# A selective-scan and FP4 feed-forward kernel: the same instructions in other slots, B rows ahead of C rows on the transfer queue

## The chip, the cores and the metric

One core of one Trainium2 chip runs the whole program. The metric is the device time in microseconds, the median of the runs shown. Engine names in the profile: PE is TensorE, DVE is VectorE, ACT is ScalarE, POOL is GpSimd, SP is SyncE, which here only issues transfers.

## The reference

A Mamba layer followed by a feed-forward layer, each with a layer norm before it and a residual after it; 16 sequences of 1024 tokens, 256 channels, f32.

```python
xz = layernorm(x) @ in_proj_w.T;  x, z = split(xz)            # 512 + 512
x = silu(causal_conv4(x) + conv_b);  xh = x as 4 heads of 128
dt_r, B, C = split(x_proj_w[h] @ xh)                          # 16 + 16 + 16 per head
delta = softplus(dt_proj_w[h] @ dt_r + dt_proj_b);  A = -exp(A_log)
s[t] = s[t-1] * exp(delta[t] * A) + (delta[t] * xh[t]) * B[t] # 16 states per channel
y[t] = sum_n s[t, n] * C[t, n];  y = (y + x * Dskip) * silu(z)
x1 = x_in + y @ out_proj_w.T
h = silu(fp4(v) @ fp4(w_gate).T) * (fp4(v) @ fp4(w_up).T)     # v = layernorm(x1), inner 704
out = x1 + fp4(h) @ fp4(w_down).T                             # fp4: blocks of 16, scaled by max/6
```

## The kernel before

**Units and tiles.** The scan work is cut into 128 units: one head (128 channels on the partitions) by 512 tokens. A unit has 16 states, and each state is one step. The norm, output and feed-forward work is cut into 128 tiles of 128 tokens. So one unit and one tile pass per 16 steps. A sequence has 8 units: four "early" ones (its first 512 tokens, whose scan starts at zero) and four "late" ones (whose scan starts at a carried state). Their VectorE scans are told apart in the profile by the operand `carry`.

**One step of the scan**, for state n (`g` counts all states): TensorE spreads B's row over the partitions into one of three PSUM banks `db` (`spread_b`, L1056), ScalarE makes the decay (`decay_of`, L486), VectorE multiplies `db` by `du` (L987) one step ahead and scans (L1008). `spread_b(g)` may write its bank only when scan g-3 is done. For the states 1, 4, 8, 11 and 14 (`BY_POOL`) the product is made by GpSimd instead (`drive`, L743): SyncE copies the B row to all partitions (`copy_b`, L404, two buffers, free again when the scan before last of its kind is done), and ScalarE puts the decay into the `db` bank. For each pair of states GpSimd multiplies the two states by C (`weigh`, L752), with the C rows copied by SyncE (`spread_c`, L392, three buffers: pair p waits for `weigh` of pair p-3). TensorE adds the products up (`sum_up`, L1071).

**The tables of slots.** Every engine runs one long loop of steps, and its `step` function lists jobs as `if w := due("scan", s):` and so on. The job is issued in the step with number s modulo 16, for the unit or tile that this many steps lie behind; jobs of one step are issued in the order of the text. Nothing else sets the order: each engine takes its list in turn and blocks on the semaphores of the job at its head. The engines' steps aren't aligned with one another except by these waits.

**Names used below.** Per unit: `in_proj` (L1186) makes x in `pbank` (two matmuls, k = 0 and 1) and z in `bank_a`; `delta` is the softplus of ScalarE (L591), and the first `in_proj` matmul waits for it since it read `pbank`; `du` (L801) is delta times the gated input, by GpSimd. Per tile: `rstd` (L733, GpSimd) makes the norm's factors, ScalarE's L581 applies the second of them, `silu_gate` (L503) comes behind it, then `delta`, then the absolute value of the second half of h (L596), which VectorE's `round_up_h` (L902) waits for. `down` (L1160) is the last matmul of the feed-forward, in three pairs.

Of the kernel before, what the change touches and what calls it, by code (L numbers as in the profile page):

```python
# [14 lines left out]
ALU = mybir.AluOpType  # L15
# [3 lines left out]
P = 128  # L19
# [122 lines left out]
def build(nc, hidden, win_t, conv_w, conv_b, xw, dtw, dt_b, a_log, dskip, wo_t, w_gate, w_up, w_down,  # L142
# [4 lines left out]
    with ExitStack() as ctx:  # L147
# [215 lines left out]
        def _(sp):  # L363
# [42 lines left out]
            def step(b, j, n):  # L406
                u, due = timetable(b, j, n)
                if t := due("post", 5):
                    wait(sp, x1_done, t.val(plus=-1))
                    sp.dma_start(xres[:, t.mod(2), :], x_tiles[t.val()]).then_inc(ld_res[t.mod(2)], 16)  # L410
                if w := due("scan", 5):
                    spread_c(w, 4)
                if w := due("scan", 0):
                    copy_b(w, 4)
                if w := due("scan", 0):
                    spread_c(w, 2)
                if t := due("norm", -16):
# [3 lines left out]
                if v := due("pre", 16):  # L421
# [5 lines left out]
                if t := due("post", 76):  # L427
                    sp.wait_ge(o_done, t.val(plus=1))
                    sp.dma_start(out_tiles[t.val()], ot[:, t.mod(2), :]).then_inc(ot_free[t.mod(2)], 16)
                if w := due("scan", 10):  # L430
                    spread_c(w, 7)
                if w := due("scan", -6):
                    copy_b(w, 1)
                if w := due("scan", 7):
                    spread_c(w, 6)
                if w := due("scan", 7):
                    copy_b(w, 14)
                if w := due("scan", -1):
                    spread_c(w, 0)
                if w := due("scan", -1):  # L440
                    spread_c(w, 1)
                if w := due("scan", 6):
                    spread_c(w, 5)
                if w := due("scan", 3):
                    copy_b(w, 8)
                if w := due("scan", 3):
                    copy_b(w, 11)
                if w := due("scan", 3):
                    spread_c(w, 3)
# [14 lines left out]
        def _(act):  # L464
# [50 lines left out]
            def step(b, j, n):  # L515
                u, due = timetable(b, j, n)
                if w := due("scan", 9):
                    decay_of(w, 15)
                if w := due("scan", 9):
                    keep_carry(w, 0)  # L520
                if w := due("scan", -7):
                    decay_of(w, 0)
                if t := due("post", 25):
                    act.wait_ge(v_norm, t.val(plus=1))
                    wait(act, h_op, t.val(2))
                    act.activation(bank_b[:, 0:DM], v2, ACT.Abs, scale=POWER).then_inc(v_abs, 1)
                if w := due("scan", 3):
                    decay_of(w, 9)
                if w := due("scan", 6):
                    decay_of(w, 10)  # L530
                if w := due("scan", 6):
                    decay_of(w, 12)
                if w := due("scan", 3):
                    decay_of(w, 4)
                if t := due("norm", 19):
# [6 lines left out]
                if t := due("post", 35):  # L542
                    silu_gate(t, 0)
                if v := due("pre", 20):
                    act.wait_ge(res_mm, v.val(2, 2))
                    wait(act, b_spread, v.val(N_DVE, -N_DVE))
                    act.activation(pieces[:, v.mod(2), :], pbank[:, :], ACT.Copy).then_inc(pieces_done, 1)
                if t := due("post", 20):
# [4 lines left out]
                                   accum_out=ve[:, 1, 0:1]).then_inc(var2_done, 1)  # L553
                if w := due("scan", 20):
# [4 lines left out]
                if due("post", 37) and not due("pre", 21):  # L559
                    act.preload_act_table_set("exp_and_others")  # L560
                if w := due("scan", 14):
                    decay_of(w, 14)
                if t := due("post", 52):
                    act.wait_ge(h_norm, t.val(plus=1))
                    wait(act, h_round, t.val(4))
                    act.wait_ge(cross_taken, min(t.val(plus=7), UNITS))
                    act.activation(cross[:, 0:HALF], hv[t.mod(2)][:, 0:HALF], ACT.Abs, scale=POWER).then_inc(h_abs, 1)
                if t := due("post", 31):
                    act.wait_ge(v_tp, t.val(plus=1))
                    wait(act, gu_mm, t.val(4))  # L570
                    act.activation(vt[:, :, :], bank_b[:, 0:DM].rearrange("p (k t) -> p k t", k=KM),
                                   ACT.Copy).then_inc(vt_done, 1)
                if t := due("norm", 15):
# [3 lines left out]
                if t := due("post", 63):  # L577
                    fetch_h(t, 0)
                if t := due("post", 20):
                    act.wait_ge(rstd_done, t.val(plus=12))  # L580
                    act.activation(v2, v2, ACT.Copy, scale=ve[:, 1, 1:2]).then_inc(v_done, 1)  # L581
                if t := due("post", 36):
                    silu_gate(t, 1)
                if w := due("scan", 20):
                    keep_carry(w, 1)
                if v := due("pre", 20):
                    h = v.mod(HEADS)
                    act.preload_act_table_set("softplus")
                    act.wait_ge(dt_mm, v.val(plus=1))
                    wait(act, du_done, v.val(plus=-1))  # L590
                    act.activation(delta[:, v.mod(2), :], pbank[:, :], ACT.Softplus,  # L591
                                   bias=dtb[:, h:h + 1]).then_inc(delta_done, 1)
                    act.preload_act_table_set("exp_and_others")
                if t := due("post", 52):
                    act.wait_ge(h_round, t.val(4, 2))
                    act.activation(cross[:, 0:HALF], hv[t.mod(2)][:, HALF:INNER], ACT.Abs, scale=POWER).then_inc(h_abs, 1)  # L596
                if w := due("scan", 7):
                    decay_of(w, 8)
                if v := due("pre", 7):
# [7 lines left out]
                    else:  # L607
                        wait(act, x_evac, v.val(2, -6))
                        act.activation(xlate[:, 0:TAPS - 1], halo[:, h, :], ACT.Copy).then_inc(x_evac, 1)
                        act.activation(xlate[:, TAPS - 1:], pbank[:, :], ACT.Copy).then_inc(x_evac, 1)  # L610
                if w := due("scan", 7):
                    decay_of(w, 13)
                if t := due("norm", -6):
# [4 lines left out]
                if w := due("scan", -6):  # L618
                    decay_of(w, 2)
                if t := due("post", 18):  # L620
                    act.wait_ge(sum2_done, t.val(plus=1))
                    wait(act, v_tp, t.val())
                    act.activation(v2, x1[:, t.mod(4), :], ACT.Identity, bias=sum2[:, 0:1],  # L623
                                   scale=-float(DM)).then_inc(centred2, 1)
                if v := due("pre", 18):
                    act.wait_ge(res_mm, v.val(2, 1))
                    act.activation(mid[:, :], pbank[:, :], ACT.Copy).then_inc(mid_done, 1)
                if w := due("scan", 2):
                    decay_of(w, 7)
                if w := due("scan", 11):  # L630
                    decay_of(w, 11)
                if t := due("norm", -5):
                    act.wait_ge(sum1_done, t.val(plus=1))
                    wait(act, xn_tp, t.val(plus=-1))
                    act.activation(xn[:, t.mod(2), 0:DM], xin[:, t.mod(2), 0:DM], ACT.Identity, bias=sum1[:, 0:1],
                                   scale=-float(DM)).then_inc(centred1, 1)
                if w := due("scan", -5):
                    decay_of(w, 3)
                if v := due("pre", 12):
# [10 lines left out]
                if w := due("scan", 0):  # L650
                    decay_of(w, 1)
                if v := due("pre", 16):
                    act.wait_ge(xd_mm, v.val(plus=1))
                    wait(act, dt_mm, v.val())
                    wait(act, res_mm, v.val(2))
                    wait(act, c_written, v.val(16))
                    wait(act, b_written, v.val(16))
# [765 lines left out]
```

## Time and profile before

| | us |
|---|---|
| median of 3 runs | 4243.98 |
| lowest and highest | 4243.51, 4249.21 |
| the profiled execution | 4253.05 |
| its span | 4251.1 |
| VectorE busy | 4060.8 (96%) |
| TensorE busy, matmuls | 3945.4 (93%) |
| GpSimd busy | 3941.9 (93%) |
| ScalarE busy | 3639.7 (86%) |

The profiled execution is one run of its own; the rows below count its span. A row of the timeline gives the start, the duration, the engine, the line and what is written from what; square brackets hold the time in which the engine had nothing to do before it, and what ended that. `x2` merges two instructions that stand next to each other. TensorE's granted clock is given as a share of full speed, 2.4 GHz.

### The profile page before, as it was taken

What the parts mean: (1) busy time and instruction counts of PE and PEld (TensorE: products, weight loads), DVE (VectorE), ACT (ScalarE), POOL (GpSimd) and SP (SyncE); (2) the same over time, 40 slices, a digit from 0 to 9 for tenths busy, and PEclk for the clock granted to TensorE, in tenths of its full rate; (3) what the DMA queues carried; (4) which work ended last, traced back from release to release, by engine and by line L of the source; (5) the groups of instructions that cost most, each with busy time, mean ns of one, the idle gap of its engine ahead of it and who ended that gap; (6) DMA issues with size and microseconds to landing.
All of it is one profiled execution on the core that took longest, in us unless ns stands there. A gap on an engine that the chain in (4) does not pass through costs nothing. (4 is left out here: it accounts for less than half of the span.)

```text
span 4251.1 us, 67554 instructions
## 1 busy us (share of the span) xinstructions
PE 3945.4 (93%) x19884; PEld 1859.3 (44%) x19884; DVE 4060.8 (96%) x5684; ACT 3639.7 (86%) x6807; POOL 3941.9 (93%) x2461
## 2 busy tenths in 40 slices
PE   4789999999999999999999999999999999999997
PEld 1234444444444444444444444444444444444445
DVE  6899999999999999999999999999999999999994
ACT  5888888888888888888888888888888888888874
POOL 5999999999999999999999999999999999999993
PEclk8999999999999999999999999999999999999999
DMA  3555555555555555555555555555555555555550
GB/s 107 200 192 192 186 187 191 186 189 188 185 187 190 188 185 191 184 189 191 188 184 191 184 187 190 185 185 190 192 183 190 188 186 190 189 186 187 183 184 23
DMA packets 307411, 772.79 MB, mean 182 GB/s; under 512 B 37734, under 2 KB 89062, under 8 KB 307046
## 3 DMA queue, kind: packets, MB, share of 16 engines
q1 hardware_dynamic: 305344, 766.31, 54.0%
q8 instruction: 162, 2.65, 0.2%
q10 hardware_dynamic: 1702, 2.16, 0.2%
q14 instruction: 203, 1.66, 0.1%
HBM read 743.16 MB, written 25.17 MB: 181 GB/s over the span
## 5 line engine op out<-in xcount | busy, mean ns | idle before, releaser
L752 POOL TENSOR_TENSOR prod<-state,cs 128x1024 f32<-128x1024 f32 x1024 | 2411.5, 2367 | 10.6 <-issue 10.3
L743 POOL TENSOR_TENSOR brow<-brow,du 128x512 f32<-128x512 f32 x640 | 817.2, 1277 | 189.6 <-DMA brow<-b_rows 179.2
L486 ACT ACTIVATE decay<-delta,aneg 128x512 f32<-128x512 f32 x1408 | 962.4, 716 | 22.5 <-DVE state L1008 20.7
L987 DVE TENSOR_TENSOR db<-db,du 128x512 f32<-128x512 f32 x1408 | 962.3, 683 | 17.8 <-PE db L1056 16.9
L1071 PE MATMUL ybank<-prod,ident 64*64 64x512 f32 x3584 | 899.3, 610 | 9.9 <-DVE hh L905 6.4
L1071 PE MATMUL cross<-prod,ident 64*64 64x512 f32 x3584 | 899.2, 610 | 0.0
L1008 DVE TENSOR_TENSOR_SCAN state<-decay,carry,db 128x512 f32<-128x512 f32 x704 | 883.1, 1263 | 0.0
L1008 DVE TENSOR_TENSOR_SCAN state<-decay,db 128x512 f32<-128x512 f32 x704 | 841.6, 1204 | 6.3 <-PE bank_b L1344 6.3
L1056 PE MATMUL db<-pieces,sel 128*128 128x512 bf16 x1408 | 541.3, 385 | 48.9 <-DVE state L1008 42.9
L486 ACT ACTIVATE db<-delta,aneg 128x512 f32<-128x512 f32 x640 | 437.8, 684 | 47.6 <-DVE state L1008 44.5
L1160 PE MATMUL bank_a<-wd,ht 128*128 128x256 f32 x1536 | 406.6, 390 | 57.7 <-ACT hh L503 56.0
L1008 DVE TENSOR_TENSOR_SCAN state<-db,carry,brow 128x512 f32<-128x512 f32 x320 | 408.1, 1275 | 9.7 <-issue 8.0
L1008 DVE TENSOR_TENSOR_SCAN state<-db,brow 128x512 f32<-128x512 f32 x320 | 388.7, 1215 | 28.4 <-issue 23.2
L1071 PEld LDWEIGHTS ybank<-prod,ident 64*64 64x64 f32 x3584 | 203.2, 133 | 472.6 <-issue 378.1
L1160 PEld LDWEIGHTS bank_a<-wd,ht 128*128 128x128 f32 x1536 | 289.3, 193 | 253.2 <-issue 223.9
L1186 PE MATMUL pbank<-xnt,win 128*128 128x512 f32 x512 | 281.2, 633 | 111.1 <-ACT delta L591 110.4
L1145 PE MATMUL bank_a<-wg,vt 128*128 128x352 f32 x1024 | 356.7, 471 | 5.2 <-DVE x L945 2.7
L1056 PEld LDWEIGHTS db<-pieces,sel 128*128 128x128 bf16 x1408 | 137.1, 97 | 505.6 <-DVE state L1008 341.1
L1112 PE MATMUL bank_b<-wu,vt 128*128 128x352 f32 x1024 | 345.5, 460 | 0.0
L581 ACT ACTIVATE v_eps<-v_eps,ve 128x256 f32<-128x256 f32 x128 | 65.2, 509 | 238.4 <-POOL ve L733 238.3
L1175 PE MATMUL bank_a<-wo,yg 128*128 128x256 f32 x1024 | 263.9, 380 | 0.0
L1112 PEld LDWEIGHTS bank_b<-wu,vt 128*128 128x128 f32 x1024 | 194.4, 190 | 134.7 <-issue 59.6
(144 smaller groups left out, 7643.7 us busy)
## 6 DMA issues: line engine op xcount, KB each, us to landing
cs<-c_rows SPq DMA_DIRECT2D x1024, 512.0 KB, 3.7
brow<-b_rows SPq DMA_DIRECT2D x640, 256.0 KB, 3.9
xin<-in_hidden SPq DMA_DIRECT2D x128, 128.0 KB, 3.8
xres<-in_hidden SPq DMA_DIRECT2D x128, 128.0 KB, 3.8
out_x<-ot SPq DMA_DIRECT2D x128, 128.0 KB, 3.9
c_rows<-xdbl SPq DMA_DIRECT2D x128, 32.0 KB, 3.4
b_rows<-xdbl SPq DMA_DIRECT2D x128, 32.0 KB, 3.2
win<-in_win_t SPq DMA_DIRECT2D x1, 1024.0 KB, 5.1
```

The lines of the kernel that those rows point to most:

```text
L486: act.activation(out, delta[:, w.mod(2), :], ACT.Exp, scale=aneg[:, w.mod(HEADS), n:n + 1]).then_inc(done, 1)
L743: pool.tensor_tensor(brow[:, s, :], brow[:, s, :], du[:, w.mod(2), :], ALU.mult).then_inc(db_pool, 1)
L752: pool.tensor_tensor(prod[:, r, :, :], state[:, 2 * p:2 * p + 2, :], cs[:, c, :, :], ALU.mult).then_inc(weighted, 1)
L987: dve.tensor_tensor(t[:, :], t[:, :], du[:, gu % 2, :], ALU.mult).then_inc(db_done, 1)
L1008: dve.tensor_tensor_scan(state[:, n, :], by, plus, start, ALU.mult, ALU.add).then_inc(scanned, 1)
L1056: pe.matmul(db[g % DB_BANKS][:, :], sel[:, gn, :], pieces[:, gu % 2, :], start=True, stop=True).then_inc(b_spread, 1)
L1071: last = pe.matmul((ybank, cross)[k][c * Q:(c + 1) * Q, :], ident[rows, rows], prod[rows, p % P_RING, k, :], start=(p == 0), stop=(k == 1 ...
L1112: last = pe.matmul(bank_b[:, 0:HALF], vt[:, k, :], wu[:, k, part * HALF:(part + 1) * HALF], start=(k == 0), stop=(k == KM - 1))
L1145: last = pe.matmul(bank_a[:, 0:HALF], vt[:, k, :], wg[:, k, part * HALF:(part + 1) * HALF], start=(k == 0), stop=(k == KM - 1))
L1160: last = pe.matmul(bank_a[:, 0:DM], ht[:, k, :], wd[:, k, :], start=(k == 0), stop=(k == KI - 1))
L1175: last = pe.matmul(bank_a[:, 0:DM], yg[:, t.mod(8) // 4, h, i * P:(i + 1) * P], wo[:, h, :], start=(h == 0), stop=(h == HEADS - 1))
L1186: return pe.matmul((pbank, bank_a)[part][:, :], win[:, k, part * DI + h * P:part * DI + (h + 1) * P], xnt[:, v.mod(8) // 4, k, :], start=( ...
```

## The change

Only the slots and the order of jobs in the tables change, on all five engines. No instruction is added or removed, and the count of steps, buffers and semaphores is the same.

A few lines of the diff stand for its kind:

```diff
# SyncE
-                if w := due("scan", 0):
-                    copy_b(w, 4)
+                if w := due("scan", -3):
+                    copy_b(w, 4)
# GpSimd
-                if v := due("pre", 26):
+                if v := due("pre", 23):
                     pool.wait_ge(delta_done, v.val(plus=1))
                     ...
-                if w := due("scan", 4):
+                if w := due("scan", 6):
                     drive(w, 8)
# TensorE
-                if v := due("pre", 6):
+                if v := due("pre", 7):
                     pe.wait_ge(xnt_done, v.div(4, 4, 4))
                     wait(pe, delta_done, v.val())
                     in_proj(v, 0, 0)
+                if v := due("pre", 7):
+                    in_proj(v, 0, 1).then_inc(x_mm, 1)
# VectorE
-                if t := due("post", 47):
+                if t := due("post", 48):
                     dve.wait_ge(h_scale, t.val(3, 2))
                     dve.reciprocal(hs[:, 1, :], hs[:, 0, :]).then_inc(h_scale, 1)
```

SyncE before, from the C rows of pair 7 (`waits weighted`, first row) to those of pair 2 of the next unit; the rows between are B row 1, the result's tile, C pairs 0 and 1, and B row 4:

```order
L392 DMA cs<-c_rows 128x1024 [waits weighted]
L404 DMA brow<-b_rows 128x512 [waits scanned,b_written]
L429 DMA out_x<-ot 128x256 [waits o_done]
L392 DMA cs<-c_rows 128x1024 [waits weighted,c_written]
L392 DMA cs<-c_rows 128x1024 [waits weighted]
L404 DMA brow<-b_rows 128x512 [waits scanned]
L392 DMA cs<-c_rows 128x1024 [waits weighted]
```

SyncE now, from B row 1 on (C pair 7 follows the result's tile, then B row 4, C pair 0, the tile of x, C pairs 1 and 2):

```order
L404 DMA brow<-b_rows 128x512 [waits scanned,b_written]
L442 DMA out_x<-ot 128x256 [waits o_done]
L392 DMA cs<-c_rows 128x1024 [waits weighted]
L404 DMA brow<-b_rows 128x512 [waits scanned]
L392 DMA cs<-c_rows 128x1024 [waits weighted,c_written]
L425 DMA xin<-in_hidden 128x256 [waits var2_done,var1_done]
L392 DMA cs<-c_rows 128x1024 [waits weighted] x2
```

B row 4 stood behind C pairs 0 and 1 of its unit, whose waits are for `weigh` of pairs 5 and 6 of the unit before; now it stands ahead of both. Likewise B row 14, which stood behind C pair 6, now stands ahead of C pairs 5 and 6.

GpSimd before, from `drive` 4 (first row) to `weigh` 3 (last row; `du` comes two places after it):

```order
L743 TENSOR_TENSOR brow<-brow,du 128x512
L770 TENSOR_TENSOR hh<-hh,hs 128x704
L752 TENSOR_TENSOR prod<-state,cs 128x1024
L733 TENSOR_TENSOR ve<-ve,minus_half 128x2
L743 TENSOR_TENSOR brow<-brow,du 128x512
L752 TENSOR_TENSOR prod<-state,cs 128x1024 x2
L743 TENSOR_TENSOR brow<-brow,du 128x512
L807 TENSOR_TENSOR v_eps<-v_eps,vs 128x256
L752 TENSOR_TENSOR prod<-state,cs 128x1024
```

GpSimd now, the same stretch:

```order
L743 TENSOR_TENSOR brow<-brow,du 128x512
L789 TENSOR_TENSOR hh<-hh,hs 128x704
L752 TENSOR_TENSOR prod<-state,cs 128x1024
L733 TENSOR_TENSOR ve<-ve,minus_half 128x2
L752 TENSOR_TENSOR prod<-state,cs 128x1024
L743 TENSOR_TENSOR brow<-brow,du 128x512
L774 TENSOR_TENSOR du<-delta,uu 128x512
L752 TENSOR_TENSOR prod<-state,cs 128x1024
L782 TENSOR_TENSOR v_eps<-v_eps,vs 128x256
L743 TENSOR_TENSOR brow<-brow,du 128x512
L752 TENSOR_TENSOR prod<-state,cs 128x1024
```

`drive` 8 moved behind `weigh` 1, `du` moved forward to directly behind it, and `drive` 11 now follows `du`, `weigh` 2 and the short product of the norm.

TensorE before, around `in_proj` into `pbank`, which waits for `delta` (the `db` rows are the spreads of states 9 and 10):

```order
L1160 MATMUL bank_a<-wd,ht 128x256 x2
L1186 MATMUL pbank<-xnt,win 128x512
L1160 MATMUL bank_a<-wd,ht 128x256 x2
L1056 MATMUL db2<-pieces,sel 128x512
L1186 MATMUL pbank<-xnt,win 128x512
L1160 MATMUL bank_a<-wd,ht 128x256 x2
L1056 MATMUL db0<-pieces,sel 128x512
```

TensorE now, the same stretch:

```order
L1160 MATMUL bank_a<-wd,ht 128x256 x2
L1186 MATMUL pbank<-xnt,win 128x512 x2
L1160 MATMUL bank_a<-wd,ht 128x256 x2
L1056 MATMUL db0<-pieces,sel 128x512
L1056 MATMUL db1<-pieces,sel 128x512
L1160 MATMUL bank_a<-wd,ht 128x256 x2
```

Both `in_proj` matmuls now stand ahead of the spread of state 9.

## Rows read from the trace of the kernel before

**Rows 1.** The page: busy time of the engines, and the group of `weigh`.
```profile
PE 3945.4 (93%) x19884; PEld 1859.3 (44%) x19884; DVE 4060.8 (96%) x5684; ACT 3639.7 (86%) x6807; POOL 3941.9 (93%) x2461
...
L752 POOL TENSOR_TENSOR prod<-state,cs 128x1024 f32<-128x1024 f32 x1024 | 2411.5, 2367 | 10.6 <-issue 10.3
```

**Rows 2.** VectorE by stretches: length, busy (count), clock, DMA share, GB/s.
```profile
0.00:300.00 300.00, 252.82 (x285) 0.92 0.52 166
300.00:3900.00 3600.00, 3520.07 (x4956) 1.00 0.56 188
4100.00:4251.00 151.00, 93.53 (x173) 0.92 0.22 71
...
2120.00:2248.00 128.00, 122.68 (x173) 0.97 0.57 187
2248.00:2376.00 128.00, 127.81 (x181) 1.00 0.56 188
```

**Rows 3.** VectorE's waits, 300 to 3900 us: total, times, longest.
```profile
DVE hw L902 <- ACT cross L596: 47.1, 78, 0.8
DVE state L1008 <- issue: 24.1, 38, 1.7
DVE db L987 <- PE db L1056: 6.4, 13, 0.8
```

**Rows 4.** GpSimd's longest wait, 300 to 3900 us.
```profile
POOL brow L743 <- DMA brow<-b_rows: 154.5, 110, 2.7
```

**Rows 5.** SyncE's issues in an early unit, timeline.
```profile
2135.51 2.59 SPq L392 DMA_DIRECT2D cs<-c_rows  x2
2138.15 0.43 SPq L404 DMA_DIRECT2D brow<-b_rows  x1
```

**Rows 6.** GpSimd in the same unit: `drive` 4 and `rstd`.
```profile
2143.00 1.27 POOL L743 TENSOR_TENSOR brow<-brow,du 128x512 f32<-128x512 f32 x1 [1.67 <-DMA brow<-b_rows]
...
2147.88 0.70 POOL L733 TENSOR_TENSOR ve<-ve,minus_half 128x2 f32<-128x2 f32 x1
```

**Rows 7.** ScalarE behind `rstd` in the same unit.
```profile
2148.61 0.51 ACT L581 ACTIVATE v_eps<-v_eps,ve 128x256 f32<-128x256 f32 x1 [2.50 <-POOL ve L733]
...
2150.89 0.69 ACT L591 ACTIVATE delta<-pbank,dtb 128x512 f32<-128x512 f32 x1
```

**Rows 8.** VectorE in that unit: scans 14 and 0, then its three waits.
```profile
2133.85 1.21 DVE L1008 TENSOR_TENSOR_SCAN state<-db,brow 128x512 f32<-128x512 f32 x1
...
2137.45 1.16 DVE L1008 TENSOR_TENSOR_SCAN state<-decay,db 128x512 f32<-128x512 f32 x1
...
2144.36 1.22 DVE L1008 TENSOR_TENSOR_SCAN state<-db,brow 128x512 f32<-128x512 f32 x1 [0.63 <-issue]
...
2153.39 0.53 DVE L902 SCALAR_TENSOR_TENSOR hw<-cross,hh 128x352 f32<-128x352 bf16 x1 [0.81 <-ACT cross L596]
...
2155.62 0.70 DVE L987 TENSOR_TENSOR db<-db,du 128x512 f32<-128x512 f32 x1 [0.85 <-PE db L1056]
```

**Rows 9.** TensorE in that unit: the matmuls that waited for `delta`.
```profile
2151.72 1.91 PE L1186 MATMUL pbank<-xnt,win 128*128 128x512 f32 x2 [1.00 <-ACT delta L591]
```

**Rows 10.** That stretch: length, busy of PE, PEld, DVE, ACT, POOL, clock, DMA.
```profile
2150.00:2158.00 8.00, 7.00 (x26) 3.75 (x28) 6.22 (x12) 6.67 (x11) 8.00 (x5) 0.79 0.53 177
```

**Rows 11.** A late unit, GpSimd: `drive` 8 and `drive` 11.
```profile
2021.48 1.27 POOL L743 TENSOR_TENSOR brow<-brow,du 128x512 f32<-128x512 f32 x1
...
2027.35 1.28 POOL L743 TENSOR_TENSOR brow<-brow,du 128x512 f32<-128x512 f32 x1
```

**Rows 12.** The same late unit, VectorE: the product of state 9, then scan 11.
```profile
2027.79 0.69 DVE L987 TENSOR_TENSOR db<-db,du 128x512 f32<-128x512 f32 x1
...
2033.77 1.27 DVE L1008 TENSOR_TENSOR_SCAN state<-db,carry,brow 128x512 f32<-128x512 f32 x1
```

**Rows 13.** The same late unit, TensorE: `in_proj` behind `delta`, the spread of state 9.
```profile
2024.55 1.10 PE L1186 MATMUL pbank<-xnt,win 128*128 128x512 f32 x2 [0.82 <-ACT delta L591]
...
2026.35 0.38 PE L1056 MATMUL db<-pieces,sel 128*128 128x512 bf16 x1
```

More of the change, by code:

```diff
@@ L516, in step @@
                 u, due = timetable(b, j, n)
[L517 to L535, printed above, removed]
+                if t := due("norm", 20):
                     act.wait_ge(xn_tp, t.val(plus=1))
@@ L558, in step @@
                     act.activation(ycross, cross[:, :], ACT.Copy).then_inc(cross_taken, 1)
[L559 to L573, printed above, removed]
+                if t := due("post", 67):
+                    fetch_h(t, 1)
+                if w := due("scan", 3):
+                    decay_of(w, 7)
+                if w := due("scan", 3):
+                    decay_of(w, 4)
+                if v := due("pre", 19):
+                    act.wait_ge(res_mm, v.val(2, 1))
+                    act.activation(mid[:, :], pbank[:, :], ACT.Copy).then_inc(mid_done, 1)
+                if w := due("scan", 0):
+                    decay_of(w, 1)
+                if t := due("norm", 16):
                     act.wait_ge(rstd_done, t.val(plus=1))
@@ L802, in step @@
                                        ALU.mult).then_inc(du_done, 1)
-                if w := due("scan", 8):
-                    drive(w, 11)
+                if w := due("scan", 5):
+                    weigh(w, 1)
+                if w := due("scan", 7):
+                    weigh(w, 2)
                 if t := due("post", 24):
@@ L809, in step @@
                 if w := due("scan", 8):
+                    drive(w, 11)
+                if t := due("post", 50):
+                    pool.wait_ge(h_scale, t.val(3, 3))
+                    hb = blocks(hv[t.mod(2)])
+                    pool.tensor_tensor(hb, hb, spread(hs[:, 1, :], INNER // BLK),
+                                       ALU.mult).then_inc(h_norm, 1)
+                if t := due("post", 58):
+                    pool.wait_ge(h_round, t.val(4, 4))
+                    hb = blocks(hv[t.mod(2)])
+                    pool.tensor_tensor(hb, hb, spread(hs[:, 0, :], INNER // BLK),
+                                       ALU.mult).then_inc(h_quant, 1)
+                if w := due("scan", 10):
+                    weigh(w, 4)
+                if w := due("scan", 3):
+                    weigh(w, 0)
+                t1, t2 = due("norm", 3), due("post", 19)
+                if t1 or t2:
+                    rstd(t1, t2)
+                if t := due("post", 28):
+                    pool.wait_ge(v_round, t.val(2, 2))
+                    pool.tensor_tensor(blocks(v2), blocks(v2), spread(vs[:, 0, :], DM // BLK),
+                                       ALU.mult).then_inc(v_quant, 1)
+                if w := due("scan", 9):
                     weigh(w, 3)
+                if w := due("scan", 1):
+                    drive(w, 4)
             def quantise(w, k):
@@ L1261, in side @@
-                if w := due("scan", 11):
-                    spread_b(w.val(NST, 13))
-                if v := due("pre", 12):
-                    in_proj(v, 1, 1).then_inc(z_mm, 1)
-                if w := due("scan", 12):
-                    sum_up(w, (2,))
-                if w := due("scan", 12):
-                    sum_up(w, (3,))
-                if t := due("post", 28):
-                    pe.wait_ge(v_quant, t.val(plus=1))
-                    if peeled and t.val() == 0:
-                        pe.wait_ge(xnt_done, 11)
-                    else:
-                        wait(pe, h_op, t.val(2))
-                    for k in range(KM):
-                        last = pe.transpose(bank_b[:, k * P:(k + 1) * P], v2_eps[:, k * P:(k + 1) * P], ident[:, :])
-                    last.then_inc(v_tp, 1)
@@ L1278, in side @@
[L1278 to L1287 removed]
+                if w := due("scan", 14):
+                    spread_b(w.val(NST, 15))
@@ new lines, in side @@
+                if v := due("pre", 14):
+                    pe.wait_ge(u_done, v.val(plus=1))
+                    pe.matmul(pbank[:, :], xws[:, v.mod(HEADS), :], uu[:, v.mod(4), :],
+                              start=True, stop=True).then_inc(xd_mm, 1)
+                if w := due("scan", -2):
+                    spread_b(w.val(NST, 0))
+                if t := due("post", 14):
+                    project(t, (1, 2, 3))
+                if w := due("scan", 9):
+                    spread_b(w.val(NST, 9))
@@ new lines, in side @@
+                if t := due("post", 64):
+                    turn_h(t, 0)
+                if w := due("scan", 16):
+                    sum_up(w, (4,))
+                if t := due("post", 71):
+                    down(t, (0, 1))
+                if v := due("pre", 7):
+                    pe.wait_ge(xnt_done, v.div(4, 4, 4))
+                    wait(pe, delta_done, v.val())
+                    in_proj(v, 0, 0)
+                if v := due("pre", 7):
+                    in_proj(v, 0, 1).then_inc(x_mm, 1)
@@ new lines, in side @@
+                if v := due("pre", 11):
+                    wait(pe, o_done, v.val(plus=-9))
+                    if v.val() < 10:
+                        wait(pe, sz_done, v.val())
+                        wait(pe, x1_done, v.val(plus=-6))
+                        wait(pe, silu_g, v.val(2, -14))
+                    in_proj(v, 1, 0)
+                if v := due("pre", 11):
+                    in_proj(v, 1, 1).then_inc(z_mm, 1)
+                if w := due("scan", 22):
+                    pe.wait_ge(cross_taken, w.val(plus=1))
+                    pe.matmul(ybank[:, :], swap[:, :], ycross, start=False, stop=True,
+                              skip_group_check=True).then_inc(joined, 1)
@@ L1314, in side @@
+                if t := due("post", 38):
+                    up(t, 1)
+                if w := due("scan", 11):
+                    sum_up(w, (2,))
+                if w := due("scan", 13):
+                    sum_up(w, (3,))
                 if t := due("post", 13):
                     project(t, (0,))
-                if w := due("scan", -3):
-                    spread_b(w.val(NST, 0))
+                if t := due("post", 29):
+                    pe.wait_ge(v_quant, t.val(plus=1))
+                    if peeled and t.val() == 0:
+                        pe.wait_ge(xnt_done, 11)
+                    else:
+                        wait(pe, h_op, t.val(2))
+                    for k in range(KM):
+                        last = pe.transpose(bank_b[:, k * P:(k + 1) * P], v2_eps[:, k * P:(k + 1) * P], ident[:, :])
+                    last.then_inc(v_tp, 1)
@@ L1319, in unit @@
+                if t := due("post", 65):
+                    turn_h(t, 1)
+                if w := due("scan", 1):
+                    spread_b(w.val(NST, 3))
             def unit(trip, j):
```

446 lines of the change are left out of this document (203 added, 243 removed).

## The prediction

> **What bounds the kernel now.** I read the page first: VectorE is busy 96% of the span, TensorE and GpSimd 93% [rows 1]. No edit removes an instruction, so a gain can only come out of VectorE's idle time, as long as VectorE stays the fullest engine. Then the stretches [rows 2]: from 300 to 3900 us VectorE works 3520.1 of 3600 us, so 79.9 us are idle there. The first 300 us hold 47.2 idle us and the last 151 us hold 57.5, both from filling and draining. The two rows of 128 us are the most telling. The one that lies mostly in early units (scans without `carry`) has 5.3 idle us in about four units, the one in late units has 0.2. Late units are full: nothing is to be had there. Early units lose 1.3 us each, and 64 of them make 85 us, which agrees with the 79.9.
>
> Next the waits of VectorE in that stretch [rows 3]: 47.1 us for ScalarE's absolute value (L596), 24.1 us at a scan that needs a GpSimd row ("issue": the profile names no releaser), 6.4 us for a spread by TensorE. Together 77.6 us. To find what starts them I followed one early unit.
>
> - SyncE issues B row 4 at 2138.15 [rows 5]. It stood behind a C transfer that waits for `weigh` of pair 6, though its own condition, scan 14 of the unit before, was met when that scan ended at 2133.85 + 1.21 = 2135.06 [rows 8].
> - GpSimd's `drive` 4 starts at 2143.00, after 1.67 us of waiting for the row [rows 6]: 4.85 us from issue to use. The wait occurs 110 times and totals 154.5 us [rows 4].
> - VectorE's scan 4 waits 0.63 us [rows 8] for it. GpSimd's `rstd` comes late by the same 1.67 us; ScalarE waits 2.50 us for it [rows 7], and everything behind on ScalarE is late: `delta`, then the absolute value, for which VectorE waits 0.81 us [rows 8].
> - TensorE waits 1.00 us for `delta`, and the two matmuls behind the wait take 1.91 us [rows 9] where the same two take 1.10 us in a late unit [rows 13]; the granted clock of that stretch is 0.79 [rows 10], a mix of the 2.4 GHz and 1.2 GHz levels, after two waits of about 1 us. So the spread of state 9 is late, and VectorE waits 0.85 us [rows 8].
>
> One late transfer thus stands at the head of all three waits.
>
> **The change part by part.**
>
> *B row 4 ahead of C pairs 0 and 1.* Its copy can go out when scan 14 ends, at about 2135.1 in that unit, since the C transfer now ahead of it (pair 7) waits for `weigh` 4, long done. With the same 4.85 us it is usable at 2139.95. GpSimd was free for it at 2143.00 - 1.67 = 2141.33. The wait of 1.67 us goes, with 1.4 us to spare. What comes late next? C pairs 0 and 1 are issued at most one issue, 0.43 us, later, and are needed two or more products later: no cost. B row 14 now waits for scan 8 ahead of C pairs 5 and 6, which are needed only by the `weigh`s after `drive` 14: no cost, and if this cover is gone it shows as a wait of `weigh` for its transfer.
>
> *GpSimd's order.* Its sum of work is the same. `drive` 8 moves behind one `weigh`, 2.37 us [rows 1]. It started at 2021.48 and ends at 2022.75, while scan 8 comes behind the product that starts at 2027.79 [rows 11, 12]: margin 5.0 us, 2.7 left. `drive` 11 ended at 2028.6 and scan 11 starts at 2033.77 [rows 11, 12]; it moves back by `du` and a short product, about 1.9 us, and 3.2 us are left. Both at nothing. `du` moves forward and now needs `delta` early: after `rstd` GpSimd has `weigh` 1 and `drive` 8, 2.37 + 1.27 = 3.6 us [rows 1, 11], before it. `delta` ended 2150.89 + 0.69 - (2147.88 + 0.70) = 3.0 us after `rstd` [rows 6, 7]. Margin 0.6 us: no cost, but thin.
>
> *TensorE's order.* Both `in_proj` matmuls now stand between `delta` and the spread of state 9. By the late unit that puts the spread about 0.9 us later behind `delta` (half of 1.10 with its overlap up to half of 1.91 at the lower clock: 0.55 to 0.96) [rows 9, 13]. The spread ended at 2026.73 and its product started at 2027.79 [rows 12, 13], a margin of 1.06 us in late units and none in early ones. But `delta` itself should come earlier against VectorE, by what GpSimd no longer waits: 1.67 us in the early unit. So the early spread gains 1.67 and gives back at most 0.96. I leave 4 of the 6.4 us of this wait in.
>
> *VectorE's order.* The reciprocal of h's scales moves from ahead of scan 0 to behind it. Scan 0 behind it took 1.16 us against 1.21 for scan 14 [rows 8]. If this small saving is lost, it costs 0.05 x 128 = 6.4 us; if it is found again elsewhere, 0. I take 3, the middle, as both are equally near. `round_up_h` of the second half now comes ahead of the gated y product, which is some 0.6 us earlier in VectorE's order, so it asks for more of ScalarE: 1.67 gained on ScalarE's chain less 0.81 that was missing and less 0.6 leaves 0.3 us to spare. I leave 8 of the 47.1 us in.
>
> *ScalarE's and the other slots.* ScalarE is busy 86% and its decays run up to six states ahead; filling and draining keep the same leads. I take 0, with -5 to +5 for the slots at the two ends, about a tenth of their 47.2 + 57.5 idle us.
>
> **The sum.** Against the profiled execution, 4253.05: the scan wait 24.1 to 2 (-22), the wait for ScalarE 47.1 to 8 (-39), the spread 6.4 to 4 (-2.4), the reciprocal +3. That makes -60.5, or 4192.6. The profiled execution is 9.1 us above the median of the runs shown, 4243.98, so the forecast there is 4183.5, rounded to 4183. All of rows 3 removed and nothing given back would be 4166; the ends -5 make it 4161.
>
> **The rivals.**
>
> *The gain is cut to half.* GpSimd needs 3941.9 / 128 = 30.8 us per unit, set-up included [rows 1], and VectorE's early unit 122.7 / 4 = 30.7 [rows 2]. Once the transfer doesn't hold it, GpSimd has nothing to catch up with, and any wait of its own reaches VectorE within the four early units. If half of the 77.6 us stay: 4244 - 39 + 3 = 4208. For it: the margins of 0.3 and 0.6 us above. Against it: late units, where VectorE needs more, give GpSimd time to get ahead again.
>
> *The wait only moves: no change.* If ScalarE takes over 0.6 us longer from `rstd` to `delta` than before, GpSimd waits at `du`. With 1 us or more of that per unit it is where it was with the transfer: 4244.
>
> *Slower, by the spread of state 9.* If `delta` doesn't come earlier against VectorE (because ScalarE's new order spends the gain), the spread is 0.55 to 0.96 us later in every unit. The early units have no margin, and 64 x 0.9 = 58 us are added: 4302; late units lie at the edge of their 1.06. It decides from a `delta` that comes less than 0.9 us earlier. For it: TensorE's waits before these matmuls come with the lower granted clock [rows 9, 10]. Against it: the source of the lateness of `delta` is the one that the change takes away. The Trainium skill, "TensorE: Matmul & The Clock Gate", section "HAM oscillation — how this bites in real kernels", says that a wait ahead of each burst of matmuls can send the array back to the low clock so that each burst starts slow; the trace agrees, with 1.91 us against 1.10. By that rule the added matmul costs its high-end price in each unit whose wait stays, and next to nothing where the wait goes.
>
> *The change doesn't do what it says.* If the B rows' 4.85 us grow with another load on the queue, `drive` 4 waits on; over 1.4 us more are needed. I count this with no change.
>
> **How the numbers follow.** Forecast (4165 to 4205) 0.60; half (4205 to 4235) 0.16, so faster 0.76. Within 0.2% (8.5 us, about what a measurement can tell) 0.10. Slower 0.14, most of it the spread at 4300. The range 4158 to 4246 leaves out the slower case and a little below.
>
> **What would show it.** GpSimd's wait for the B rows falls from 154.5 us to under 30; ScalarE's wait for `rstd` in early units from 2.5 us to under 1; VectorE's waits in 300 to 3900 us from 77.6 to about 14, and early stretches of 128 us reach 127 busy. VectorE's wait for the spread stays under 10 us; if it rises to 50 or more, the last rival holds. A new wait of GpSimd at `du` for `delta` is the second rival. The prediction is wrong if late stretches of VectorE show over 1 us idle per 128 us, since I count on their staying full.

## The result and the profile after

The changed kernel takes 4139.17 us (median of 4 runs, 4136.59 to 4141.37) against 4243.74 us for the kernel before (four runs, one more than in the table above): ratio 0.9755, 95% interval 0.9738 to 0.9772. It is faster, as forecast, but by 104.6 us instead of 60.5, and below the range given. The profiled execution took 4136.59 us, its span is 4134.7 us, 116.4 us less than before. The two profiled executions lie farther apart than the medians, since the one of the kernel before was 9 us above its median.

VectorE by stretches (columns as in [rows 2]):

```profile
0.00:300.00 300.00, 259.19 (x295) 0.94 0.53 170
300.00:3900.00 3600.00, 3599.88 (x5091) 1.00 0.58 193
3900.00:4134.70 234.70, 184.01 (x299) 0.98 0.35 116
```

The engines' busy time and the group of `weigh` on the page, which answer to [rows 1]:

```profile
PE 3878.1 (94%) x19569; PEld 1898.4 (46%) x19884; DVE 4043.1 (98%) x5684; ACT 3683.0 (89%) x6807; POOL 3944.6 (95%) x2461
...
L752 POOL TENSOR_TENSOR prod<-state,cs 128x1024 f32<-128x1024 f32 x1024 | 2417.8, 2367 | 13.5 <-DVE state L1008 13.5
```

The 3878.1 us of TensorE can't be set against the 3945.4 of before: 315 of its 19884 matmuls, all of them spreads of B, have no record in this trace.

VectorE, which was idle for 79.9 us between 300 and 3900 us, is idle for 0.1 us there. Its busy time fell too, by 17.7 us, with the same 5684 instructions; that is taken up below.

The waits of VectorE and of GpSimd from 300 to 3900 us, all that the view lists (answering to [rows 3, 4]):

```profile
DVE db L987 <- remote: 0.9, 1, 0.9
```

```profile
POOL v_eps L782 <- DVE vs L955: 33.2, 67, 0.7
POOL v_eps L805 <- DVE v_eps L905: 29.6, 78, 1.1
POOL ve L733 <- issue: 0.5, 3, 0.2
POOL brow L743 <- DMA brow<-b_rows: 0.5, 2, 0.3
```

GpSimd's wait for the B rows fell from 154.5 us to 0.5. It now waits for VectorE, at the two short products of the norm: GpSimd is the engine that is ahead.

One early unit, the answer to [rows 5 to 8]: SyncE's issue of B row 4, GpSimd's `drive` 4 and `rstd`, ScalarE's L607 (the same operation as L581 before) and `delta`, VectorE's second `round_up_h` and the product of state 9.

```profile
2081.09 0.32 SPq L404 DMA_DIRECT2D brow<-b_rows  x1
...
2085.80 1.29 POOL L743 TENSOR_TENSOR brow<-brow,du 128x512 f32<-128x512 f32 x1
...
2090.69 0.70 POOL L733 TENSOR_TENSOR ve<-ve,minus_half 128x2 f32<-128x2 f32 x1
...
2091.63 0.49 ACT L607 ACTIVATE v_eps<-v_eps,ve 128x256 f32<-128x256 f32 x1
...
2093.78 0.69 ACT L615 ACTIVATE delta<-pbank,dtb 128x512 f32<-128x512 f32 x1
...
2097.03 0.52 DVE L902 SCALAR_TENSOR_TENSOR hw<-cross,hh 128x352 f32<-128x352 bf16 x1
...
2099.02 0.70 DVE L987 TENSOR_TENSOR db<-db,du 128x512 f32<-128x512 f32 x1
```

None of them has a bracket: nobody in the chain waits. ScalarE's wait for `rstd`, 214.3 us in 110 waits from 300 to 3900 us before, is not in the list of its waits any more. TensorE in the same stretch runs the four parts of both `in_proj` matmuls in 1.88 us at full clock, where before two parts took 1.91 us at a granted clock of 0.79 [rows 9, 10]:

```profile
2095.20 1.88 PE L1186 MATMUL pbank<-xnt,win 128*128 128x512 f32 x4
```

and the stretch around it (columns as in [rows 10]):

```profile
2092.00:2100.00 8.00, 7.87 (x34) 4.70 (x36) 8.00 (x16) 7.71 (x15) 8.00 (x6) 1.00 0.54 179
```

### The profile page after: what moved, and what is told of

Its sections match the earlier page's. It is cut to its first block and busy times, and to the rows that moved or that the text cites. A ratio compares the mean times of both kernels' runs of the same rounds, so it can differ in the third digit from the quotient of the medians.

```text
span 4134.7 us, 67240 instructions
## 1 busy us (share of the span) xinstructions
PE 3878.1 (94%) x19569; PEld 1898.4 (46%) x19884; DVE 4043.1 (98%) x5684; ACT 3683.0 (89%) x6807; POOL 3944.6 (95%) x2461
## 5 line engine op out<-in xcount | busy, mean ns | idle before, releaser
L486 ACT ACTIVATE decay<-delta,aneg 128x512 f32<-128x512 f32 x1408 | 973.0, 711 | 16.2 <-DVE state L1008 16.0
L1071 PE MATMUL ybank<-prod,ident 64*64 64x512 f32 x3584 | 882.5, 603 | 34.1 <-DVE hh L905 18.6
L1071 PE MATMUL cross<-prod,ident 64*64 64x512 f32 x3584 | 882.5, 604 | 0.0
L1056 PE MATMUL db<-pieces,sel 128*128 128x512 bf16 x1093 | 408.7, 383 | 85.3 <-DVE state L1008 79.8
L1160 PE MATMUL bank_a<-wd,ht 128*128 128x256 f32 x1536 | 393.1, 380 | 1.2 <-ACT ht L511 1.2
L1112 PE MATMUL bank_b<-wu,vt 128*128 128x352 f32 x1024 | 356.4, 470 | 1.1 <-DVE hh L912 0.9
L1145 PE MATMUL bank_a<-wg,vt 128*128 128x352 f32 x1024 | 346.3, 461 | 1.5 <-DVE x L959 1.1
L1175 PE MATMUL bank_a<-wo,yg 128*128 128x256 f32 x1024 | 277.1, 393 | 2.8 <-DVE ot L973 2.4
L1112 PEld LDWEIGHTS bank_b<-wu,vt 128*128 128x128 f32 x1024 | 184.5, 190 | 166.8 <-DVE hh L912 91.5
L1186 PE MATMUL bank_a<-xnt,win 128*128 128x512 f32 x512 | 252.9, 616 | 6.4
L1175 PEld LDWEIGHTS bank_a<-wo,yg 128*128 128x128 f32 x1024 | 184.2, 190 | 162.0 <-issue 145.3
```

The lines of the kernel that those rows point to most:

```text
L486: act.activation(out, delta[:, w.mod(2), :], ACT.Exp, scale=aneg[:, w.mod(HEADS), n:n + 1]).then_inc(done, 1)
L1056: pe.matmul(db[g % DB_BANKS][:, :], sel[:, gn, :], pieces[:, gu % 2, :], start=True, stop=True).then_inc(b_spread, 1)
L1071: last = pe.matmul((ybank, cross)[k][c * Q:(c + 1) * Q, :], ident[rows, rows], prod[rows, p % P_RING, k, :], start=(p == 0), stop=(k == 1 ...
L1112: last = pe.matmul(bank_b[:, 0:HALF], vt[:, k, :], wu[:, k, part * HALF:(part + 1) * HALF], start=(k == 0), stop=(k == KM - 1))
L1145: last = pe.matmul(bank_a[:, 0:HALF], vt[:, k, :], wg[:, k, part * HALF:(part + 1) * HALF], start=(k == 0), stop=(k == KM - 1))
L1160: last = pe.matmul(bank_a[:, 0:DM], ht[:, k, :], wd[:, k, :], start=(k == 0), stop=(k == KI - 1))
```

## The experiments

The variants ran on three chips (column "chip"); the chip of the first comparison is not on record. On these three the kernel before takes 4265.0 to 4273.9 us (medians of four groups of runs), so each variant is compared with the kernel before of its own group by the ratio. The changed kernel itself ran again on chip 2 only, with 4139.61 us, close to the 4139.17 of the first comparison; differences in us between runs on different chips lean on that.

| run | what differs | chip | median us | ratio to before (95%) |
|---|---|---|---|---|
| after_again | the changed kernel | 2 | 4139.61 | 0.9698 (0.9683 to 0.9712) |
| e1_b4_ahead | before, B row 4 ahead | 2 | 4142.58 | 0.9697 (0.9682 to 0.9711) |
| e9_b4_between | before, B row 4 one place less far | 2 | 4145.70 | 0.9709 (0.9695 to 0.9724) |
| e8_drive4_later | before, GpSimd's job moved instead | 2 | 4153.75 | 0.9730 (0.9711 to 0.9750) |
| e2_sp_table | before, SyncE's new table | 2 | 4134.12 | 0.9673 (0.9658 to 0.9687) |
| e3_b4_back | changed, B row 4 put back | 2 | 4331.55 | 1.0135 (1.0120 to 1.0150) |
| e5_inproj_ahead | before, `in_proj` moved | 2 | 4273.67 | 1.0000 (0.9991 to 1.0010) |
| e6_inproj_behind | changed, `in_proj` put back | 12 | 4141.14 | 0.9710 (0.9686 to 0.9734) |
| e7_dve_before | changed, VectorE's old table | 2 | 4132.11 | 0.9678 (0.9664 to 0.9693) |
| e11_in_order | e7 again | 14 | 4133.87 | 0.9680 (0.9667 to 0.9694) |
| e10_recip_back | changed, reciprocal put back | 14 | 4135.11 | 0.9684 (0.9670 to 0.9697) |

### Is the late transfer the cause? e1, e9, e8, e3

e1, the kernel before with one number changed:

```diff
-                if w := due("scan", 0):
+                if w := due("scan", -3):
                     copy_b(w, 4)
```

> The kernel before with one slot changed: B row 4 is issued at slot -3 (ahead of C pairs 0 and 1) and nothing else. Theory 'one late transfer': GpSimd's wait for the B rows falls from 154.5 us (300 to 3900) to under 30, VectorE's 77.6 us of waits to under 15, and the time is 4140 to 4165, most of the 104 us. Rival 'the tables together': the order of GpSimd and ScalarE is what brings rstd and delta in time, so VectorE's wait at L902 (47 us) stays over half and the time is 4190 to 4225. Rival 'another row takes its place': the wait of GpSimd moves to B row 1, 8 or 14 and the time stays within 10 us of 4244.

4142.58 us: within 3 us of the changed kernel. VectorE's waits from 300 to 3900 us, then GpSimd's longest:

```profile
DVE state L1008 <- issue: 0.7, 3, 0.4
```

```profile
POOL ve L733 <- ACT xin L552: 24.4, 55, 0.8
POOL brow L743 <- DMA brow<-b_rows: 23.7, 43, 1.5
```

All three waits of VectorE are gone with one transfer, so they were one stall, and the tables of the other engines weren't needed for it.

e9 puts the row between C pairs 0 and 1 (slot -1, text between the two), so it waits for `weigh` 5 instead of 6.

> The kernel before with B row 4 issued between C pairs 0 and 1, so it waits for weigh 5 instead of weigh 6, 2.3 us earlier than before and later than in the run with B row 4 ahead of both. Theory: the wait of 0.9 to 1.7 us is covered by 2.3 us, so the gain is nearly whole, within 10 us of that run's 4142.6. Rival 'every microsecond of the row's earliness counts': a part of the gain only, 4180 to 4220.

4145.70 us: 2.3 us of earliness are enough for nearly the whole gain, where the waits were 1.4 us on average (154.5 us in 110) and 2.7 at the longest [rows 4]. More of it adds next to nothing: GpSimd's waits for the B rows are 26.4 us here and 23.7 in e1.

e8 leaves SyncE alone and moves GpSimd's job so that it works while the row is under way:

```diff
                 if t := due("post", 50):
                     ...
+                if w := due("scan", 2):
+                    drive(w, 4)
                 ...
-                if w := due("scan", -1):
-                    drive(w, 4)
```

> The kernel before with one slot of GpSimd changed and SyncE's table untouched: drive 4 stands behind the scaling of h (1.4 us), so that GpSimd works while the row of B is on its way. Theory 'the late row costs through GpSimd's idle time, which delays rstd, delta and the absolute value': GpSimd's wait falls by 1.3 us per unit, VectorE's waits at L902 and L987 go, its wait at scan 4 (24 us) stays, and the ratio to before is 0.975 to 0.985. Rival 'the row itself is what VectorE lacks': no gain, ratio 0.995 to 1.01, since the row lands no earlier.

4153.75 us, ratio 0.973, a little more gain than expected. GpSimd's wait for B rows is 43.5 us and VectorE's are these:

```profile
DVE state L1008 <- issue: 8.3, 16, 1.3
DVE db L987 <- PE db L1056: 0.9, 1, 0.9
```

SyncE's table is as before, the row is still issued behind the C rows that wait for `weigh` 6, and most of the gain is there. So the cost ran through GpSimd's idle time and what was queued behind it (`rstd`), not through the scan that needs the row. I had expected that scan's own wait to stay at 24 us, and only 8.3 are left. That this is because GpSimd, and with it SyncE, now runs ahead is likely but wasn't tested.

e3 undoes the one slot in the changed kernel (B row 4 behind C pair 1 again).

> The changed kernel with B row 4 put back behind C pair 1 (slot 0), nothing else. Theory 'one late transfer': the wait of GpSimd at drive 4 comes back, but the rest of the order has margins of 1 us and more that hide part of it; drive 4 now stands behind weigh 6 and 7 one after the other, so the row is late by about 1.0 to 1.7 us per unit and the time is 4190 to 4245. Rival 'the tables together': under 4160, the other tables carry the gain.

4331.55 us, 1.35% slower than the kernel before and far worse than the 4190 to 4245 expected. SyncE, then GpSimd with its wait:

```profile
2117.89 0.32 SPq L392 DMA_DIRECT2D cs<-c_rows  x1
2118.26 0.42 SPq L404 DMA_DIRECT2D brow<-b_rows  x1
...
2122.30 1.27 POOL L743 TENSOR_TENSOR brow<-brow,du 128x512 f32<-128x512 f32 x1 [2.13 <-DMA brow<-b_rows]
```

In the changed kernel `drive` 1 no longer stands between `weigh` 6 and `drive` 4, so the transfer has only `weigh` 7 for cover. Its wait is 2.13 us, and VectorE's wait at L902 grows to this (300 to 3900 us):

```profile
DVE hw L902 <- ACT cross L620: 133.1, 111, 1.5
DVE state L1008 <- issue: 13.9, 35, 1.5
```

GpSimd's new order is therefore safe only together with SyncE's. The two changes aren't a sum of two gains.

### Do the other tables add anything? e2, e6, e7, e10, e11

e2 is the kernel before with SyncE's whole new table.

> The kernel before with the whole table of SyncE taken from the changed kernel, the other four engines as before. Theory 'one late transfer': as e1 or better by up to 5 us, 4140 to 4165. Rival 'the tables together': the new SyncE order is made for the new GpSimd order; B row 8, which GpSimd before needs right behind rstd, now stands behind C pair 2 and the rows' write as it did, B row 14 comes earlier; time 4190 or more.

4134.12 us, 5.5 us better than the changed kernel, with VectorE busy all 3600 us between 300 and 3900. So the new tables of the four other engines, taken together, cost a little time.

after_again is the reference on chip 2.

> The changed kernel as it is, on the chip of this group of runs, so that the variants can be set beside it: 4136 to 4142 if its time doesn't hang on the chip as the time of the kernel before does.

e7 is the changed kernel with VectorE's old table.

> The changed kernel with VectorE's table of the kernel before (the reciprocal of h's scales ahead of scan 0, y's product ahead of scan 7). Theory 'VectorE is the bound and only its own order counts now': the reciprocal's place is worth 0.05 us per unit, 6 us, so 4130 to 4135, with VectorE still at no waits. Rival 'the tables fit one another': TensorE's and ScalarE's new slots are made for VectorE's new ones, and the mixture waits again, 4150 or more.

4132.11 us. This and e2 agree within 2 us, though ScalarE, GpSimd and TensorE have the new order in one and the old in the other. Where VectorE is full, only its own order counts. At the two ends it isn't full, and the other slots count there: e1 too has VectorE's old table and lists 0.7 us of waits from 300 to 3900 us, yet it takes 4142.58. Set side by side instruction by instruction, the profiled executions of e1 and e2 differ by 8.8 us, of which 7.8 lie outside 300 to 3900 us. The repetition of e7, beside e10:

> The changed kernel with VectorE's table of the kernel before, once more beside the run with the reciprocal alone: 4128 to 4134 again. If the reciprocal explains all of it, the two agree within 2 us.

4133.87 us. e10 puts back only the reciprocal:

```diff
-                if t := due("post", 48):
+                if t := due("post", 47):
                     dve.wait_ge(h_scale, t.val(3, 2))
                     dve.reciprocal(hs[:, 1, :], hs[:, 0, :]).then_inc(h_scale, 1)
```

> The changed kernel with only the reciprocal of h's scales put back ahead of scan 0 (slot 47). VectorE has no waits in the changed kernel, so only start-to-start times count. Theory: the scan behind the reciprocal starts its successor 0.06 to 0.09 us sooner than other scans, 128 times, so 4130 to 4134, the whole gain of the run with VectorE's old table (4132.1). Rival: the gain of that run lay in y's product and the other jobs' places; then this one stays at 4137 to 4141.

4135.11 us, a little above the 4130 to 4134 given, and 1.2 us above e11 of the same group: the two agree within 2 us, so the reciprocal's place explains nearly all of what VectorE's old table is worth. That is 4.5 us against the changed kernel's 4139.61, of 5.7 (e11) and 7.5 (e7). The timelines show where. Before, a late unit (reciprocal, scan 0, then the next product):

```profile
2011.46 0.41 DVE L949 RECIPROCAL hs<-hs 128x44 f32<-128x44 f32 x1
2011.79 1.18 DVE L1008 TENSOR_TENSOR_SCAN state<-decay,carry,db 128x512 f32<-128x512 f32 x1
2012.89 0.67 DVE L987 TENSOR_TENSOR db<-db,du 128x512 f32<-128x512 f32 x1
```

After, the same three in the new order:

```profile
2020.86 1.28 DVE L1008 TENSOR_TENSOR_SCAN state<-decay,carry,db 128x512 f32<-128x512 f32 x1
2022.05 0.41 DVE L965 RECIPROCAL hs<-hs 128x44 f32<-128x44 f32 x1
2022.37 0.68 DVE L987 TENSOR_TENSOR db<-db,du 128x512 f32<-128x512 f32 x1
```

The scan takes 1.10 us to the next start when it stands behind the reciprocal and 1.19 us when it doesn't, and the reciprocal's own cost hardly changes (0.33 and 0.32). The two together take 1.43 us before and 1.51 after in late units. In early units it is 1.41 and 1.45 (medians, 300 to 3900 us). With the third digit, that makes 64 x (0.074 + 0.034) = 6.9 us. The profiled executions agree: from the start of the first scan to the end of the last one it is 3958.2 us in the changed kernel and 3951.8 in e10, 6.4 less. The runs as a whole show 4.5, and what lies outside those scans varies by more than the difference: it is 176.5 and 179.5 us in the two profiled executions of the changed kernel, and 181.5 in e10.

### The rival at the spread of state 9: e5, e6

e5 moves only TensorE's second `in_proj` matmul ahead, in the kernel before, where `delta` is late:

```diff
-                if v := due("pre", 7):
-                    in_proj(v, 0, 1).then_inc(x_mm, 1)
                 if v := due("pre", 6):
                     ...
                     in_proj(v, 0, 0)
+                if v := due("pre", 6):
+                    in_proj(v, 0, 1).then_inc(x_mm, 1)
```

> The kernel before with only TensorE's second in_proj matmul (k = 1) moved directly behind the first, ahead of down (2, 3) and the spread of state 9, as the changed kernel has it. My slower rival: delta is as late as before, so the spread of state 9 comes 0.55 to 0.96 us later in each unit, VectorE's wait for it grows from 6.4 to 50 us or more, 4290 to 4310. Theory that this place has a margin even then: within 10 us of 4244.

4273.67 against 4273.86 us: no change, so the rival falls, with its premise granted (`delta` as late as before). VectorE's waits from 300 to 3900 us:

```profile
DVE hw L902 <- ACT cross L596: 54.1, 90, 0.8
DVE state L1008 <- issue: 19.8, 46, 1.7
DVE db L987 <- PE db L1056: 15.4, 9, 1.7
```

The wait for the spread is 15.4 us, in 9 places only. One of them, TensorE and VectorE:

```profile
2167.05 3.55 PE L1186 MATMUL pbank<-xnt,win 128*128 128x512 f32 x4 [1.00 <-ACT delta L591]
...
2168.72 0.53 DVE L902 SCALAR_TENSOR_TENSOR hw<-cross,hh 128x352 f32<-128x352 bf16 x1 [0.80 <-ACT cross L596]
...
2171.82 0.70 DVE L987 TENSOR_TENSOR db<-db,du 128x512 f32<-128x512 f32 x1 [1.71 <-PE db L1056]
```

Here the four parts took 3.55 us, at the low clock; at the full clock they take 1.88 to 1.96. All nine waits are such places, each of 1.71 us, where the unit of [rows 8] had 0.85: in these nine the 0.9 us that I had priced is there. But the low clock is rare. TensorE waited 108 times for `delta` in this stretch, and the matmuls behind ran at the full clock in 99 of them. In the kernel before it was 6 of some 105, and the late unit of [rows 13] had shown it: 1.10 us right behind a wait of 0.82. All nine had a second wait of 0.77 to 1.05 us some 2 us earlier (0.94 in the rows above), but so had 23 others that stayed at the full clock. What decides between them isn't shown.

Where the matmuls run at the full clock nothing is lost, because VectorE is late by the same cause: it waits for the absolute value behind `delta` and has three operations, that one and two more, before the product. Both branches start at `delta`, and I had charged one with the lateness and left the other on time. That the early units had no margin here I had read from one unit with the low clock; [rows 3] has only 13 waits for the spread in all.

e6 puts the matmul back behind the spread in the changed kernel.

> The changed kernel with TensorE's second in_proj matmul put back behind the spread of state 9. Theory: with no waits on VectorE this place has over 1 us of margin either way, so within 4 us of 4139. Rival: the new place was needed for the gain, since x is evacuated and its taps start earlier; then over 4150.

4141.14 us, 1.5 us from 4139.61, within the spread of the runs (on another chip): the place is worth nothing there either that these runs could tell.

### Why does the kernel before take some 25 us more than in the first comparison? before_again

> The kernel before as it is, profiled on a chip where its time is some 4269 to 4274 and not 4244, while the changed kernel takes 4139 on both. Theory: all of the difference lies in the stall that starts at B row 4, which grows with the time from issue to landing; GpSimd's wait for the B rows is 170 to 200 us from 300 to 3900 us instead of 154.5, and VectorE's three waits are 95 to 105 instead of 77.6. Rival: the waits are as before, and the instructions themselves last longer on this chip, VectorE busy over 4080 us.

Inconclusive. This execution took 4259.33 us, below the others of this chip. Its waits are close to those of the first profile, with 161.2 us for GpSimd's B rows:

```profile
DVE hw L902 <- ACT cross L596: 44.0, 76, 0.8
DVE state L1008 <- issue: 20.9, 34, 1.6
DVE db L987 <- PE db L1056: 9.4, 20, 1.2
DVE db L987 <- remote: 7.2, 14, 1.2
```

They sum to 81.5 us against 77.6, and VectorE is busy 4062.4 us against 4060.8. Neither theory shows 25 us, and these two executions can't: the first profiled one took 4253.05 us, so they are 6.3 us apart and not 25. What stays: the kernel that stalls took 4243.7 us in the first comparison and 4265.0 to 4273.9 in the four groups after it, and the one that doesn't took 4139.2 and 4139.6. Whether the chip makes the difference isn't shown, and the cause is open.

## Why the prediction was right and wrong

**The mechanism was right.** The one late transfer headed all three waits. e1 and e8 show it from two sides and e3 shows the reverse. The margins that the prediction worked out held: `du` behind `delta` has no wait, C rows behind B rows have none, `drive` 8 and 11 neither.

**The size was wrong, and the step that failed is the sum.** Its terms against the two profiled executions, 116.4 us apart (the medians are 104.6 apart, and there the sum falls short by 44):

- Waits from 300 to 3900 us: I took 63 of 77.6 us away and left 14, for margins that I called thin. All of the 79.9 idle us but 0.1 went. Short by 16 us.
- Outside 300 to 3900 us: I took 0, with -5 to +5 for the slots. VectorE's idle time there went from 110.4 to 91.5 us. Short by 19 us. The stall accounts for a part: with B row 4 alone (e1) 103.6 are left, 7 less. The other 12 came with the other slots, and 4.5 of them are draining: from the start of the last late scan to the end of the span it is 98.9 us before, 97.4 in e1 and 92.9 after.
- VectorE's busy time: I had +3 us for the reciprocal, and it fell by 17.7 us. Short by 21 us. With VectorE's order unchanged it falls by 23 (4060.8 to 4037.7 us in e1 and 4037.5 in e7), so the new order costs 6 of it back, where I had 3. Nothing about the instructions changed. In the trace of the kernel before a scan's record overlaps its successor by some 0.09 us when nothing waits (a scan of 1.21 us, the next start after 1.13). An instruction that waited doesn't show this overlap, and one that was late by less than it leaves no gap to list; the shortest bracket of VectorE in this trace is 0.15 us. The kernel before and e1 have the same 5684 VectorE instructions in the same order, so each can be compared from its start to the next start. From 300 to 3900 us the 129 with a bracket before cost 88.8 us more than in e1, for 77.7 us of brackets, and another 139 without one cost 11.2 us more. So a wait costs its bracket and some 0.09 us, and short ones cost time that no view lists. This makes up 21 of the 23 us; the other 2 lie at the two ends.

The three make 56, which is 116.4 less 60.5. The floor that I gave, "all of rows 3 removed", 4166, was no floor for the same reasons: it took the brackets for the whole cost.

**Late units.** I took them for full, from one stretch of 128 us with 0.2 us idle [rows 2]. That reading was wrong, and its agreement with the 79.9 us (64 early units at 1.3 us) was luck; the sum doesn't hang on it, since it took the waits as totals. Other stretches of the kernel before that hold mostly late units have 1.9 and 1.6 us idle (columns as in [rows 2]):

```profile
1224.00:1352.00 128.00, 126.11 (x177) 1.00 0.55 186
1480.00:1608.00 128.00, 126.39 (x177) 1.00 0.55 187
```

Some 20 of the 77.6 us of waits stand in late units, and the 110 waits for a B row [rows 4] are about one for each of the 112 units of that stretch, early or late. From one gated y product to the next a late unit took 32.01 us on average before (31.53 where nothing waited) and takes 31.60 now; an early one took 31.91 and takes 30.63 (units at the change from one kind to the other left out). The unit of [rows 8], with 33.16 (2150.52 to 2183.68), is among the worst. After the change the late stretches are full, as the prediction's last sign asks.

**The rivals.** "Half" and "only moves" fell: GpSimd kept its lead, and its waits for VectorE show why it does: 62.8 us of reserve between 300 and 3900 us. "Slower" fell by its own mechanism in e5: it put 0.9 us on each of 64 units, and nine places paid it. The Trainium skill, "TensorE: Matmul & The Clock Gate", section "HAM oscillation — how this bites in real kernels", tells of waits behind which every burst of matmuls starts at the low clock. This trace agrees in nine of e5's 108 waits for `delta` and not in the other 99, where the four parts took 1.95 us.

**A better version.** e7 is the fastest, 4132.11 and 4133.87 us in two groups of runs, and e2 takes 4134.12: both keep VectorE's old order. Their runs don't overlap those of the changed kernel on chip 2 (4138.95 to 4141.24); the slowest of e11, 4137.17, is just above the fastest of the first comparison, 4136.59.

## What to carry to other kernels

When the fullest engine shows several kinds of short waits, follow one period back to the first engine that idles: here one transfer, queued behind two others whose waits it didn't need, started all of them, and one number moved was worth 3%. Price a stall from start to start, as the average of many periods against undisturbed ones, not by its brackets and not from one period: a single stretch made late units look full here. Before pricing a low clock, count how often it comes. When a stall makes one branch late, take it that the branch it is compared with may be late by the same cause.

## What the runs showed of the hardware

The recorded length of a VectorE instruction isn't its cost. The scans of early units that take the decay from its own tile have a median of 1210 ns in the kernel before, 1303 in e1 and 1395 in e7, while two scans in a row take 2.24 us from start to start in all three (2205.46 to 2207.70, 2120.53 to 2122.77, 2116.98 to 2119.22). Only starts can be compared between executions.
